# Two-layer residual kernel, f32: the first pass stores seven left operands of each weight matrix, the second loads them in pairs

## The reference

```python
x = x + x @ w_eff.T            # layer 0: w_eff is a quantised 1024 x 1024 weight plus a LoRA delta
gate = x @ W_gate.T + 0.5 * lora(x, A_gate[i], B_gate[i])    # layer 1: 2752 rows
up   = x @ W_up.T   + 0.5 * lora(x, A_up[i],   B_up[i])
act  = silu(gate) * up
x = x + act @ W_down.T + 0.5 * lora(act, A_down[i], B_down[i])
```

## Time and profile before

| | |
|---|---|
| median of 3 runs | 1626.21 us (1625.12 to 1626.38) |
| profiled execution | 1627.25 us |
| its span, first to last instruction | 1625.6 us |
| mean granted TensorE clock | 0.992 |
| busy: PE, PEld, DVE, ACT, POOL | 97%, 80%, 76%, 35%, 33% |
| DMA | 281.26 MB, mean 173 GB/s |

### The profile page before, as it was taken

How to read it: one execution, slowest core, us unless ns; L and a number is a source line. 1 busy time by engine, 2 the same in 40 slices (tenths; PEclk the granted TensorE clock), 3 DMA queues, 4 the chain that set the end, 5 groups by cost and what they waited for, 6 DMA issues and landing times.

```text
span 1625.6 us, 21138 instructions
## 1 busy us (share of the span) xinstructions
PE 1580.1 (97%) x6968; PEld 1297.8 (80%) x6968; DVE 1243.3 (76%) x1587; ACT 563.5 (35%) x990; POOL 536.6 (33%) x401
## 2 busy tenths in 40 slices
PE   6999998899999999997999999999999999999999
PEld 4888876788888888875888888888888888888887
DVE  6998949788889988889977888878676576695353
ACT  5411125333333333353433333333343333233231
POOL 4320013364555555554353555555410000000000
PEclk9999999999999999999999999999999999999999
DMA  9461173577787888883334666665267677686563
GB/s 286 119 120 62 65 220 87 136 211 213 204 217 205 221 221 229 226 297 113 102 121 128 181 183 181 177 185 155 84 192 203 162 188 185 152 224 206 156 189 119
DMA packets 368461, 281.26 MB, mean 173 GB/s; under 512 B 225120, under 2 KB 266848, under 8 KB 368224
## 3 DMA queue, kind: packets, MB, share of 16 engines
q1 hardware_dynamic: 284480, 245.04, 53.2%
q10 hardware_dynamic: 81792, 29.05, 7.0%
q0 software_dynamic: 2080, 5.80, 1.7%
HBM read 166.27 MB, written 110.85 MB: 170 GB/s over the span
## 4 chain that ended last, share of the span: by engine, by line
PE 68%; DVE 6%; SPq 4%; DMA 2%; issue 1%; POOL 0%; ACT 0%; DVEq 0%; POOLq 0%
PE bank L1830 16%; PE bankC L1830 11%; PE bankA L1830 11%; PE bank L2057 9%; PE bankC L2057 6%; PE bankA L2057 6%; PE bankT L2057 3%; DVE rl L1323 1%; DVE xl L1332 1%; PE bankT L1873 1%; PE bankT L1874 1%; PE bankC L1846 1%; SPq L589 1%; SPq L549 1%; SPq L487 1%
## 5 line engine op out<-in xcount | busy, mean ns | idle before, releaser
L1017 ACT CAST rh<-wt 128x512 fp32r<-128x512 f32 x253 | 156.2, 620 | 379.6 <-PE bankC L1846 79.2
L1323 DVE TENSOR_TENSOR rl<-wt,rh 128x512 fp32r<-128x512 f32 x253 | 236.8, 942 | 21.8 <-ACT rh L1017 21.5
L1501 DVE TENSOR_TENSOR opl<-opl,oph 128x512 fp32r<-128x512 f32 (+1 forms) x154 | 107.9, 702 | 154.8 <-ACT oph L1131 154.6
L1830 PE MATMUL bank<-xh,rh 128*128 128x512 f32 x528 | 206.3, 391 | 2.3 <-issue 2.3
L1830 PE MATMUL bank<-xl,rh 128*128 128x512 f32 x528 | 206.1, 390 | 0.0
L1830 PE MATMUL bank<-xh,rl 128*128 128x512 f32 x528 | 206.1, 390 | 0.0
L1131 ACT CAST oph<-opl 128x512 fp32r<-128x512 f32 (+1 forms) x154 | 95.5, 621 | 268.8 <-DMA opl<-LT_d 263.7
L1830 PE MATMUL bankC<-xh,rh 128*128 128x512 f32 x352 | 138.9, 395 | 3.6 <-DVE xl L1332 2.6
L1830 PE MATMUL bankC<-xl,rh 128*128 128x512 f32 x352 | 138.7, 394 | 0.0
L1830 PE MATMUL bankA<-xh,rl 128*128 128x512 f32 x352 | 138.4, 393 | 0.0
L1830 PE MATMUL bankC<-xh,rl 128*128 128x512 f32 x352 | 138.4, 393 | 0.0
(11 more groups left out here) (217 smaller groups left out, 3671.6 us busy)
## 6 DMA issues: line engine op xcount, KB each, us to landing
opl<-LT_d SPq DMA_DIRECT2D x148, 256.0 KB, 2.9
WT_d<-wt SPq DMA_DIRECT2D x88, 256.0 KB, 3.4
RT_d<-dt SPq DMA_DIRECT2D x70, 256.0 KB, 3.2
opl<-RT_d SPq DMA_DIRECT2D x70, 256.0 KB, 3.6
LT_d<-ev ACTq DMA_DIRECT2D x60, 256.0 KB, 3.2
wb<-WT_d SPq DMA_DIRECT2D x44, 256.0 KB, 3.5
wt<-WT_d SPq DMA_DIRECT2D x44, 256.0 KB, 4.2
dn<-in_L_cond_W_down_dram SPq DMA_DIRECT2D x86, 128.0 KB, 3.9
```

Of the source, the lines that this page charges most:

```text
L1017: nc.scalar.copy(rh[:, v % RING, 0:KH * rows], wsrc(mm, RSRC[p])).then_inc(s_hi, 1)
L1323: dv.tensor_tensor(rl[:, v % RING, 0:KH * rows], wsrc(mm, RSRC[p]), rh[:, v % RING, 0:KH * rows].bitcast(f32), ALU.subtract).then_inc(s_lo, 1)
L1501: dv.tensor_tensor(opl[0:rows, L_AT[n % NL], :], opl[0:rows, L_AT[n % NL], :].bitcast(f32), oph[0:rows, L_AT[n % NL], :].bitcast(f32), ALU ...
L1830: last = te.matmul(OUT[p], a[:, u % RING, cols], b[:, OPND[p], k, :], start=k == 0 and n == 0, stop=k == KH - 1 and n == 2 and (p in (0, 1 ...
```

## The change

- **Forms.** `WT_d` (four transposes for each matrix) becomes `FT_d` (seven forms for each matrix of pass 1). SP stores each form once it is ready: in loop p = 1 form 6 of the matrix and form 0 of the next, at 3 form 5, at 4 forms 2 and 4, at 5 forms 1 and 3. The stores signal three semaphores: `s_f12` for form 2 (raw L12), `s_f4` for form 6, `s_fa` for the other five. w_tr(mm, 0) waits for all `s_fa` stores of earlier matrices, w_tr(mm, 3) for form 6 of the one before, w_s4 for its form 2; w_s3 waits for no store.
- **Pass 2** makes no sums on POOL. SP loads two forms with one DMA into a ring `wq` of ten slots, which lies over `wn` and `wt`; pair k is loaded in loop 154 + 2k - 11 or later, once lo has read what was in the slots.
- **The adapters' columns** of pass 2 need seven forms too: POOL makes four sums of them (`a_sums`, mm = 6), and store_wa has 14 strided stores instead of 8.
- **The short block's LoRA.** No ts_mask: ts_hi and ts_lo multiply by the mask themselves, in two halves of 256 tokens. Two of the four short products for each matrix now add into the banks of products 5 and 6 before these are taken (`ride_lora`, two products later: take(mm, 6) moves there); the other two come two products after that, and one late_add of 96 x 1024 takes both. store_bs waits for the matmul, not for the addition. a_hi, a_lo and td of the following blocks move by one to three loops.
- **Entering pass 1:** ACT makes hi(2), b_hi(0), hi(3), hi(4) and load_wa(1) before x_hi(0, 0); VectorE's differences are in the order T1, T2, T4, T3, and T3 comes after two x_lo. store_form(2) and load_wn(1) stand ahead of the other five stores.
- **The start:** the four lb loads move from ACT's queue to SP's, behind cb and ahead of lora_A; the split of lora_A moves behind the codebook's constants on VectorE.

```diff
+    FT_d = dram("FT_d", [2 * NJ * 7, P, KD // 2 * P], f32)
+        RIDE = {8: 0, 14: 1}
+        LATE = {10: 0, 16: 1}
+        wq = place("wq", [P, NQ, KH * P], f32, S0 + 20480)
...
+        def form(v):
+            return wt[:, RSRC[v % 7], :] if v < 7 * NH else wq[:, (v - 7 * NH) % NQ, :]
...
+                def store_form(v):
+                    form_ready(sp, v)
+                    sp.dma_start(FT_d[v, :, :], form(v)).then_inc({2: s_f12, 6: s_f4}.get(v % 7, s_fa), 16)
...
+                    if pair >= 2:
+                        sp.wait_ge(s_lo, 7 * NH + max(0, 2 * (pair - len(s_wl)) + 2))
+                    sp.dma_start(wq[:, v % NQ:v % NQ + 2, :], FT_d[v:v + 2, :, :].rearrange("k p n -> p k n")).then_inc(s_wl[pair % len(s_wl)], 16)
...
                     if it % NJ == 1:
-                        sp.wait_ge(s_lad, 8 * (it // NJ) + 4 * (g + 1))
+                        sp.wait_ge(s_fl, 4 * (it // NJ) + 2 * g + 2)
...
-                    if p in (1, 2, 3, 4) and mm + 1 < NH:
-                        store_wt(mm + 1, p - 1)
+                    if p == 1 and mm < NH:
+                        store_form(7 * mm + 6)
+                    for n in {1: (0,), 3: (5,), 4: (2, 4), 5: (1, 3)}.get(p, ()):
+                        if mm + 1 < NH:
+                            store_form(7 * (mm + 1) + n)
...
                 def w_s3(mm):
-                    if mm < NH:
-                        gp.wait_ge(s_wst[1], 16 * (mm + 1))
...
                 def w_s4(mm):
+                    gp.wait_ge(s_f12, 16 * (mm + 1))
...
-                    if n in (0, 2):
-                        wait(dve, s_wst[n], 16 * mm)
+                    if n == 0:
+                        wait(dve, s_fa, 80 * mm)
+                    if n == 3:
+                        wait(dve, s_f4, 16 * mm)
...
+                def late_add(h, m):
+                    dve.wait_ge(s_fl, 4 * h + 2 * m + 2)
+                    dve.wait_ge(s_ev, 4 * 2 * NJ * h + 4 * (m + 1))
+                    e = ev[0:FH, m, 0:4:3, :]
...
-                    dve_tail(u, (5, 7, 9) if first(it - 1) else (1, 5, 8) if it == NJ else (1, 4, 7))
+                    dve_tail(u, (6, 8, 10) if first(it - 1) else (4, 6, 9) if it == NJ else (1, 4, 7))
...
-                    td_at(u, (5, 7, 9, 11) if first(it - 1) else (0, 4, 7, 10) if it == NJ else (0, 3, 6, 9))
+                    td_at(u, (6, 8, 10, 12) if first(it - 1) else (2, 5, 8, 11) if it == NJ else (0, 3, 6, 9))
```

More of the change, by code:

```diff
@@ L396, in cond_resid_kernel @@
         s_wa = sem("p1_wa", st)
-        s_wst = [sem(f"p1_wst{i}", st) for i in range(4)]
-        s_wl = [sem(f"p1_wl{i}", st) for i in range(2)]
+        s_fa = sem("p1_fa", st)
+        s_f12 = sem("p1_f12", st)
+        s_f4 = sem("p1_f4", st)
+        s_wl = [sem(f"p1_wl{i}", st) for i in range(NQ // 2)]
         s_wat = sem("p1_wat", st)
@@ L507, in store_wa @@
                 def store_wa():
[L508 to L510 removed]
+                    sp.wait_ge(s_z, 7)
+                    sp.wait_ge(s_fa, 80 * 2)
+                    sp.wait_ge(s_f12, 16 * 2)
+                    sp.wait_ge(s_f4, 16 * 2)
                     for m in range(2):
[L512 to L516 removed]
+                        for p in range(7):
+                            src = (a_of[:, m, 0, 0, :], asum[:, 1, m, :], a_of[:, m, 0, 1, :], asum[:, 2, m, :],
+                                   asum[:, 0, m, :], a_of[:, m, 1, 1, :], asum[:, 3, m, :])[p]
+                            sp.dma_start(FT_d[7 * m + p, :, :].rearrange("p (k r) -> p k r", r=P)[:, :, FH:P],
+                                         src.rearrange("p (k r) -> p k r", r=Q)).then_inc(s_wal, 16)
@@ L761, in _ @@
                 load_raw(1, KH, KD - 1, 6, s_x[6])
-                for n in range(4):
-                    store_wt(0, n)
+                store_form(2)
                 load_wn(1)
+                for p in (0, 5, 4, 1, 3):
+                    store_form(p)
                 store_bd(KD - 1)
@@ L787, in _ @@
                         store_bs(it + 1, 0)
-                    if p in (1, 2, 3, 4) and mm + 1 < NH:
-                        store_wt(mm + 1, p - 1)
+                    if p == 1 and mm < NH:
[3 more added lines that the diff above has]
+                            store_form(7 * (mm + 1) + n)
                     if p == 3 and mm + 2 < NH:
                         load_wn(mm + 2)
-                    if p == 5 and NH <= mm + 2 < NM:
-                        load_wt(mm + 2)
+                    for pair in range(7 * NH // 2):
+                        if u == 7 * NH + max(2 * pair - 11, (-11, -9, -3, -3, -2)[min(pair, 4)]):
+                            load_forms(pair)
                     if (mm, p) == (7, 1):
@@ L1068, in ts_hi @@
                         stored(act, NORD)
-                    mine = tx[2 * CR:3 * CR, :]
-                    nc.scalar.copy(ts[2 * CR:3 * CR, t, m, :], mine).then_inc(s_th, 1)
-                    nc.scalar.copy(ts[0:CR, t, m, :], mine).then_inc(s_ts, 1)
+                    for rows, signal in ((slice(FH, P), s_th), (slice(0, CR), s_ts)):
+                        for b in range(CB):
+                            cols = slice(b * SEQ, (b + 1) * SEQ)
+                            ins = nc.scalar.activation(ts[rows, t, m, cols], ev[FH:P, m, 3 * t, cols], ACT.Copy, scale=half_of[FH:P, b:b + 1])
+                        ins.then_inc(signal, 1)
                 def td_copy(h):
@@ L1221, in _ @@
                 load_wa(1)
+                x_hi(0, 0)
+                bd_copy(KD - 1)
                 out_x1(TURN[KD - 2, 2])
@@ L1243, in _ @@
                         a_hi(4 * it)
-                    if 0 <= it - 1 < NIT and first(it - 1) and (m, p) == (0, 2):
+                    if 0 <= it - 1 < NIT and first(it - 1) and (m, p) == (0, 3):
                         a_hi(4 * (it - 1))
@@ L1470, in dn_tr @@
                     wait(dve, s_dst[(0, 1, 3, 2)[b]], 16 * rd)
+                    if b == 0:
+                        wait(dve, s_ds, 4 * rd - 1)
                     if rd == 5:
@@ L1693, in _ @@
                 x_lo(0, 0)
-                for n in range(1, 4):
-                    x_sum(n)
+                x_sum(1)
+                x_sum(2)
                 w_tr(1, 0)
@@ L1699, in _ @@
                 x_lo(0, 2)
+                x_sum(3)
                 for u in range(END):
@@ L1775, in _ @@
                         else:
-                            if p in (2, 3, 4, 6):
+                            if p in (2, 3, 4) or p == 6 and not first(it):
                                 take(mm, p)
@@ L1779, in _ @@
                                 gated(it, p // 2 - 1)
-                            if first(it) and p in (3, 5):
-                                ts_mask(h, m, p // 5)
                     for x_ in SPLIT.get(u, ()):
```

258 lines of the change are left out of this document (120 added, 138 removed).

## The result

| | before | changed |
|---|---|---|
| median | 1625.66 us (1624.51 to 1626.38, 4 runs) | 1658.87 us (1657.69 to 1663.43, 4 runs) |
| ratio | | 1.0204, 95% interval 1.0186 to 1.0223 |
| profiled execution, span | 1627.25, 1625.6 us | 1659.28, 1657.6 us |
| DMA | 281.26 MB, mean 173 GB/s | 316.24 MB, mean 191 GB/s |

The change costs 33 us. The forecast was 1632 us with a range of 1612 to 1646: right in direction, 27 us too low, and outside the range.

What follows compares the result with a forecast made beforehand. TensorE (PE), busy 97%, was taken as the bound, so only its waits counted. Gains of -18.2 and +24 inside pass 1 made +5.8 on 1627.25 us, 1633.0, less 1.04 to the median: 1632 us, range 1624 to 1640, outer 1612 to 1646.

Steps and rivals of the forecast that it cites:

- The start, -1.8: Kernel start: four lb loads leave ACT's queue for SP's, so PE's first transpose of x comes up to 1.8 us earlier.
- The end of layer 0, -5.4: End of the first layer: w_s3 no longer waits for a WT_d store, so all 5.4 us lost there go.
- Entering pass 1, -6.5: Entry of pass 1: masks, late additions and a take wait go, a wait of w_tr(1,0) comes; net gain 6.5 us.
- Inside pass 1, +24: Pass 1: transposes wait for form stores and delay a_lo and PE; 22.6 us plus 1.4 for one slowed product.
- There are nine such boundaries: Pass 1 after the entry: nine matrix boundaries wait for late stores, the largest 9.8 us, a middle one 3.2.
- The landing of 3.4 us: Pass 1: time a WT_d store was taken to need to land, used to date the late transposes.
- Three more stores ... bring no work to PE, DVE or ACT: Pass 1: three more stores for each matrix cost only SP, 0.45 us each.
- rival A: Pass 1: form stores are hidden by slack, loss 0 to 3 us, 1608 to 1611 us; chance 0.22.
- Entering pass 2, -4.5: Entry of pass 2: POOL's sums of weight blocks go and no longer slow VectorE; net gain 4.5 us.
- Pass 2 and after, 0: Inside pass 2 and after: larger loads are hidden and POOL's freed time is worth nothing; 0 us.
- B: Pass 1: SP's lag is paid once, +10 us, giving 1618 us; chance 0.20.
- C: Slow end: pass 1 boundaries as forecast but both entries give nothing, 1643 us; chance 0.12.

Runs made afterwards that it cites:

- E6: The changed kernel with the weights' way of the kernel before (four raw blocks stored, POOL's sums in pass 2) and raw L21 of matrix 0 stored first: 1618.6 us.
- E12: E11 with the adapter products, their differences and sums in pass 2's first block at the positions of the kernel before: 1603.1 us.
- E11: E6 with act_sum 3 of the first block on POOL, and its store on SP, one position earlier: 1611.0 us.
- E2: The kernel before with three more 256 KB stores for each matrix from 4 on, which nobody waits for: 1642.3 us.
- E5: The kernel before with three extra stores for each matrix, as in E2, but of 2 KB each: 1629.9 us.
- E9: E2 with the W_down loads of pass 1 taken in 4 KB pieces instead of 128 bytes: 1630.4 us.
- E13: The changed kernel with the adapter products, their differences and sums in pass 2's first block at the positions of the kernel before: 1654.0 us.
- E3: The changed kernel with forms 1 and 3 stored at SP's position 4, ahead of load_bn, load_an and xt_store: 1656.3 us.
- E4: The changed kernel with store_wa's 14 stores spread one by one over the positions of matrices 7 and 8: 1657.6 us.

## Why the prediction was wrong, step by step

- **The start, -1.8: the size fits, the way to it was another.** PE's first transpose of x comes 0.3 us earlier, not 1.8 (16.41 against 16.70), and it no longer waits for x. It stands behind a product that waits for `lbT`:

```profile
14.53 2.08 PE L1922 MATMUL bank<-la,lbT 128*128 128x512 f32 x4 [7.27 <-DVE lbT L1548]
16.41 1.05 PE L1941 MATMUL bankA<-ident,nat 128*128 128x128 f32 x4
```

  VectorE makes `lbT` behind the split of lora_A, whose load landed for it only at 11.89 us. So moving the lb loads and the split was not free, as I had put it; 8 us later (at 24 us) PE is 1.8 us ahead of the kernel before. That is within what traces of the same instructions differ by.
- **The end of layer 0, -5.4: right.** Both terms together, 7.2, stand against 7.3 in the ledger at matrix 0. PE's 3.75 us are gone, and so are the 13.75 us that w_s3 stood for a store; POOL now stands 12.18 us in w_s4, for its form 2, and PE doesn't wait for it. E6 shows that this gain doesn't need stored operands.
- **Entering pass 1, -6.5: wrong in sign.** From matrix 0 to 5 the changed kernel loses 1.8 us. What I counted as removed was there, and was worth more than I took: E12 gains 11.9 by the same place. Two things stood against it. The wait of a transpose for the form stores, which I had priced at 4 and put on w_tr(1, 0), came at w_tr(3, 0), 6.97 us, with PE behind it in a late LoRA product, 2.92 us; by the ledgers at matrix 3 it is worth about 4. And the moved act_sum 3, 7.0 us of PE and 2 more of slowed matmuls behind it, was not in my sum at all. I had listed that a_hi, a_lo and td move by one to three loops, not their sums, and costed only what was removed. E11 gives its price, 7.6 us.
- **Inside pass 1, +24: too small; it was +39.5.** "There are nine such boundaries" is the step that failed first. The boundaries that I had in view cost 22.4 us together (I had said 24), store_wa's 12.2 (9.8), the others about 1.5 each (3.2). But the transposes of the even matrices wait for stores as well, and those boundaries cost 17.1 us. I had worked with SP's order alone, which is kind to them. The landing of 3.4 us from the earlier trace rows was the second failure: a median over all 88 stores. Measured, it was 2.0 to 2.8 at the ones and mostly 4.6 to 7.0 at the others. (The one slowed product that I added at 1.4 us was 2.2 by my own reading of the earlier trace rows; that changes little.)
- **"Three more stores ... bring no work to PE, DVE or ACT": the deepest failure.** I gave them 0.45 us each on SP and put the consequence at nothing. E2 measures it at 15.4 us, with nobody waiting for the stores, and E5 at 4 us for stores of 2 KB. The loads of the weights, which PE's chain needs, stand behind them in SP's order, and SP was busy issuing for 152.7 of 189.2 us beside W_down already, at a DMA share of 0.84. I read that as slack (rival A). E9 shows that the cost needs the short pieces of W_down; whether they cost on SP or on the DMA engines stays open.
- **Entering pass 2, -4.5: too large; it was -1.8.** The gain from POOL's missing sums may be of the size that I took: with the old positions, E13 goes 7.5 us down from matrix 21 to 24. I had seen that the second a_lo goes behind x_lo of the last operand and set it off inside one number, without a term. It costs 5 us (E13), 8 in E12's pair.
- **Pass 2 and after, 0: right.** 374.93 us as before, and 424.89 against 425.00.
- **The rivals.** B ("the lag is paid once") doesn't hold: every boundary pays. But E3 and E4 show that what one boundary is spared comes back in part at the next ones; my argument that each pays because store_bs waits for PE didn't tell the two apart. C was nearest with 1643, for a part of the right reason: the entries gave nothing. No case had the traffic.

## What to carry to other kernels

Price an added store twice, in the busiest stretch that it meets: by the share of the time in which its queue's engine is already issuing, with what stands behind it in that order, and by the DMA engines' share with the GB/s beside it. Here three stores on top of 0.81 of SP's time and a DMA share of 0.84 at 225 GB/s cost 15 us. The DMA share alone doesn't tell, for E9 ran at 0.87 and lost nothing in that stretch. When a wait is shared by several stores or several steps move by a position, list every place where it is met, both parities of a loop included, and give each moved instruction its own term. And test the parts apart: here one part cost more than 40 us, and two moved positions hid what the rest was worth.

## What the runs showed of the hardware that I had not expected

- Three more stores of 256 KB for each of 18 matrices, which nobody waits for, cost 15.4 us (E2), and only 4 to 5 when the loads beside them come in 4 KB pieces instead of 128 bytes (E9). With short pieces the engines are busy 0.90 of the stretch at 251 GB/s, with long ones 0.87 at 264.
- SP was busy for 0.79 us with the issue of one load of W_down in 128-byte pieces, and for 0.48 us when the same bytes came in 4 KB pieces (E9); for 0.52 us with a 256 KB store (E2), and 0.33 with one of 2 KB (E5).
- The same store of 256 KB is seen by its waiter 2.0 to 2.8 us after its issue where the loads of the weights have landed before it is issued, and mostly 4.6 to 7.0 where they are still on their way or only just in.
